# A graph-attention and mixture-of-experts kernel: the tridiagonal recursion inside the chunks in four pair products instead of eight steps

## What is computed

```python
v = jnp.clip(ffn_out @ Wv + bv, -V_MAX, V_MAX)      # one value for each of the 128 nodes
# diagonal of (T - i)^-1, T tridiagonal with v on the diagonal and 1 beside it:
#   a_i = d_i - 1/a_{i-1} (forwards), b_i = d_i - 1/b_{i+1} (backwards), d_i = v_i - 1j
#   G_ii = 1 / (a_i + b_i - d_i)
gr, gi = _bk_gii(v)
feats = jnp.clip(jnp.stack([gr, gi], -1) * mask[..., None], -FEAT_CLAMP, FEAT_CLAMP)
return ffn_out + bk_scale * (feats @ Wo + bo)
```

## Time and profile before

| | us |
|---|---|
| median of 3 runs | 501.85 |
| lowest and highest run | 500.89, 502.28 |
| the profiled execution, its time | 502.62 |
| the profiled execution, span from first to last instruction | 500.8 |
| TensorE busy | 466.2 (93%) |
| VectorE busy | 136.2 (27%) |
| bytes read from HBM | 189.62 MB, 379 GB/s over the span |

### The profile page before, as it was taken

One profiled execution on the slowest core, in us unless ns is written; L12 is line 12 of the kernel. 1 busy time (PEld: TensorE's weight loads), 2 busy tenths in 40 slices (PEclk: granted clock), 3 DMA queues, 4 the chain that ended last, 5 costly groups with the idle time before them and its releaser, 6 DMA issues.

```text
span 500.8 us, 5998 instructions
## 1 busy us (share of the span) xinstructions
PE 466.2 (93%) x2292; PEld 232.7 (46%) x2292; DVE 136.2 (27%) x362; ACT 62.1 (12%) x119; POOL 32.9 (7%) x52
## 2 busy tenths in 40 slices
PE   7999999999998999999999999999898889789892
PEld 6666665666556344344344344353243234224352
DVE  6673697437105311010010010010010011001165
ACT  1010222002003120020020020020020011002100
POOL 3242220000100000121000000000000000000000
PEclk9999999999998999999999999999999999999996
DMA  8889999999999699899999999999999999999800
GB/s 309 309 285 403 402 401 417 413 401 411 426 425 370 237 407 375 338 417 420 425 428 423 422 427 427 423 421 430 424 424 424 425 425 423 425 425 424 347 1 31
DMA packets 32541, 190.22 MB, mean 380 GB/s; under 512 B 5423, under 2 KB 5631, under 8 KB 18190
## 3 DMA queue, kind: packets, MB, share of 16 engines
q1 hardware_dynamic: 31694, 189.94, 93.2%
q0 software_dynamic: 544, 0.05, 0.1%
q10 hardware_dynamic: 288, 0.03, 0.0%
HBM read 189.62 MB, written 0.39 MB: 379 GB/s over the span
## 4 chain that ended last, share of the span: by engine, by line
PE 58%; DMA 22%; SPq 13%; DVE 5%; issue 2%; ACT 0%; DVEq 0%
PE ps L1300 16%; DMA chunk<-in_L_ffn_W 14%; PE ps L1273 14%; PE ps L1099 11%; PE ps L1059 6%; DMA lower<-in_L_ffn_W 6%; SPq L333 5%; SPq L323 4%; SPq L328 3%; PE ps L1286 2%; PE ps L1087 2%; DMA slot<-in_L_gnn_W 2%; PE ps L1114 2%; PE ps L1235 2%; SPq L347 1%
## 5 line engine op out<-in xcount | busy, mean ns | idle before, releaser
L1300 PE MATMUL ps<-lower,hidden 128*64 128x384 f32 x516 | 88.6, 490 | 5.3 <-DMA lower<-in_L_ffn_W 5.3
L1273 PE MATMUL ps<-chunk,gathered 128*64 128x512 f32 x324 | 73.5, 598 | 7.3 <-DMA chunk<-in_L_ffn_W 7.3
L1059 PE MATMUL ps<-slot,xT 128*128 128x384 f32 x192 | 64.0, 487 | 0.2 <-DMA slot<-in_L_gnn_W 0.2
L1273 PE MATMUL ps<-extra,gathered 128*64 128x512 f32 x252 | 57.6, 597 | 6.1 <-DMA extra<-in_L_ffn_W 5.9
L1300 PEld LDWEIGHTS ps<-lower,hidden 128*64 128x64 f32 x516 | 35.9, 137 | 51.2 <-issue 40.6
L1099 PE MATMUL ps<-slot,eluT 128*128 128x384 f32 x168 | 55.3, 486 | 0.0
L884 DVE TENSOR_TENSOR hidden<-ps,b_T 128x384 f32<-128x384 f32 x32 | 17.1, 555 | 129.8 <-PE ps L1286 129.8
L1059 PEld LDWEIGHTS ps<-slot,xT 128*128 128x128 f32 x192 | 35.6, 190 | 22.8 <-issue 0.3
L1273 PEld LDWEIGHTS ps<-chunk,gathered 128*64 128x64 f32 x324 | 21.7, 136 | 50.6 <-issue 36.7
L1300 PE MATMUL ps<-lower_on,hidden 128*64 128x384 f32 x252 | 43.7, 492 | 0.0
L1099 PEld LDWEIGHTS ps<-slot,eluT 128*128 128x128 f32 x168 | 31.5, 190 | 20.7
(11 more groups left out here) (303 smaller groups left out, 287.1 us busy)
## 6 DMA issues: line engine op xcount, KB each, us to landing
lower<-in_L_ffn_W SPq DMA_DIRECT2D x43, 1152.0 KB, 23.1
chunk<-in_L_ffn_W SPq DMA_DIRECT2D x27, 1536.0 KB, 19.7
slot<-in_L_gnn_W SPq DMA_DIRECT2D x31, 1152.0 KB, 15.6
extra<-in_L_ffn_W SPq DMA_DIRECT2D x21, 1536.0 KB, 25.1
lower_on<-in_L_ffn_W SPq DMA_DIRECT2D x21, 1152.0 KB, 28.7
slot<-in_L_gnn_W SPq DMA_DIRECT2D x3, 384.0 KB, 4.8
x_sb<-in_x SPq DMA_DIRECT2D x1, 384.0 KB, 3.4
out<-xc SPq DMA_DIRECT2D x1, 384.0 KB, 2.3
```

The costliest lines, as they stand in the source:

```text
L1059: last = T.matmul(ps[:, 2 * (h % 2) + b, 0:HB], xT[:, 3 * half + k, :], slots[n % RING][:, k, b * HB:(b + 1) * HB], start=(n % 2 == 0 and ...
L1273: last = T.matmul(ps[b * CAP:(b + 1) * CAP, s, 0:BANK], gathered[:, k, :], upper_homes[k][:, at:at + BANK], start=(k == 0), stop=(k == KT ...
L1300: last = T.matmul(ps[c * CAP:(c + 1) * CAP, 4, 0:HB], hidden[:, q, k, b, :], lower_homes[i][:, k, c * HB:(c + 1) * HB], start=(i == 0 and ...
```

## The change

The tile `cf_w` shrinks from 40 to 8 elements a row. Row pairs of it now hold a 4x4 state matrix: pair 0 is the identity, written by GpSimd. For each pair of steps a 4x4 matrix K is built from the two values v0 and v1, in `cf_k` (4 matrices of 16): its constant entries are set by GpSimd's MEMSETs, its other entries by six VectorE instructions, each for all four pairs at once. Then three times a product (TENSOR_TENSOR, 48 x 64, broadcast over four) and a sum (TENSOR_REDUCE to 48 x 16) multiply K on the state; state 1 is the first K itself, copied into `cf_w` while the first product runs. The wait on `cf_init` goes from 3 to 4. `WARM[10]`, the number of identity products ahead of L1380, goes from 8 to 2.

```diff
--- before.py
+++ after.py
@@ -55,7 +55,7 @@
 LOADS = CHUNKS + DOWN
 EARLY = 3
 ATONCE = 6
-WARM = (3, 5, 2, 2, 2, 0, 1, 3, 2, 0, 8, 12)
+WARM = (3, 5, 2, 2, 2, 0, 1, 3, 2, 0, 2, 12)
 
 
 def gnn_moe_kernel(nc, x, src, dst, gw1, gas1, gad1, gb1, gw2, gas2, gad2, gb2,
@@ -127,15 +127,15 @@
         wo_rows = place("wo_rows", [P, 2, D])
         wv_row = place("wv_row", [P, D])
         top[0] = moe_base + lower_at[7]
-        tail_tiles = [("cf_w", [CP, CL + 2, 4 * (CL + 2)]), ("cf_v", [CP, CL]), ("cf_t", [CP, 4 * (CL + 2)]),
+        tail_tiles = [("cf_w", [CP, CL + 2, 8]), ("cf_v", [CP, CL]), ("cf_t", [CP, 4, 4, 4]),
               ("cf_m", [CP, CH, 16]), ("cf_mm", [2, CH, 16]), ("cf_s", [2, CH, 4]), ("cf_x", [2, 4, 4]),
               ("cf_n", [2, CH]), ("cf_p", [CP, CH, 4]), ("cf_b", [CP, 4]), ("cf_y", [CP, CL + 1, 2, 4]),
               ("cf_th", [CP, CL + 1, 2]), ("cf_q", [CP, 3, CL, 2]), ("cf_r", [CP, CL]), ("cf_a", [CP, CL, 2]),
               ("cf_d", [CH, CL, 2]), ("cf_c", [CH, CL, 2]), ("cf_g", [CH, CL, 2]), ("cf_e", [CH, CL]),
               ("cf_f", [P, CL, 2]), ("cf_pre", [2, GC, GC, 4, 4]), ("cf_px", [2, GC, 4, 2, 4]),
-              ("cf_sx", [2, GC, GC - 1, 4, 4])]
+              ("cf_sx", [2, GC, GC - 1, 4, 4]), ("cf_k", [CP, CL // 2, 16]), ("cf_h", [CP, CL // 2])]
         (cf_w, cf_v, cf_t, cf_m, cf_mm, cf_s, cf_x, cf_n, cf_p, cf_b, cf_y, cf_th, cf_q, cf_r, cf_a,
-         cf_d, cf_c, cf_g, cf_e, cf_f, cf_pre, cf_px, cf_sx) = [place(*t) for t in tail_tiles]
+         cf_d, cf_c, cf_g, cf_e, cf_f, cf_pre, cf_px, cf_sx, cf_k, cf_h) = [place(*t) for t in tail_tiles]
         assert top[0] <= moe_base + lower_at[7] + slot
         top[0] = after_moe
 
@@ -449,13 +449,14 @@
                 pool.dma_start(wo_rows[0:1, j, :], wo[j:j + 1, :]).then_inc(end_rows_in, 16)
             pool.dma_start(wv_row[0:1, :], wv).then_inc(end_rows_in, 16)
             G.memset(cf_w[:, 0:2, :], 0.0).then_inc(cf_init, 1)
+            G.memset(cf_k[:, :, :], 0.0).then_inc(cf_init, 1)
             G.memset(cf_s[:, 0, :], 0.0).then_inc(cf_init, 1)
             G.memset(cf_d[:, :, 1], -1.0)
-            pool.wait_ge(cf_init, 2)
-            for at in range(2):
-                for row, sign in ((0, 1.0), (1, 1.0), (2, -1.0), (3, -1.0)):
-                    first = 4 * row + 2 * at + row % 2
-                    G.memset(cf_w[:, at, first::16], sign)
+            pool.wait_ge(cf_init, 3)
+            G.memset(cf_w[:, 0:2, :].rearrange("p s m -> p (s m)")[:, 0::5], 1.0)
+            G.memset(cf_k[:, :, 0:6:5], -1.0)
+            G.memset(cf_k[:, :, 6:10:3], -1.0)
+            G.memset(cf_k[:, :, 3:13:9], 1.0)
             G.memset(cf_s[:, 0, 0:1], 1.0 / FAR)
             G.memset(cf_s[:, 0, 2:3], 1.0).then_inc(cf_init, 1)
 
@@ -922,14 +923,31 @@
             V.scalar_tensor_tensor(out=v_steps[:, :], in0=ps[:, 3, 0:1].to_broadcast([P, CL]), scalar=col(VBASE),
                                    in1=step_mask[:, :], op0=ALU.add, op1=ALU.mult).then_inc(v_ready, 1)
 
-            dve.wait_ge(cf_init, 3)
+            dve.wait_ge(cf_init, 4)
             dve.wait_ge(v_turned, 1)
             step(V.tensor_scalar(cf_v[:, :], ps[0:CP, 2, 0:CL], VMAX, -VMAX, ALU.min, ALU.max))
-            for i in range(CL):
-                n = 4 * (CL + 1 - i)
-                step(V.tensor_tensor(cf_t[:, 0:n], cf_w[:, i + 1, 4:4 + n], cf_w[:, i, 0:n], ALU.subtract))
-                step(V.scalar_tensor_tensor(out=cf_w[:, i + 2, 0:n], in0=cf_w[:, i + 1, 0:n],
-                                            scalar=cf_v[:, i:i + 1], in1=cf_t[:, 0:n], op0=ALU.mult, op1=ALU.add))
+            pair = [CP, CL // 2, 2]
+            v0, v1 = cf_v[:, 0:CL:2], cf_v[:, 1:CL:2]
+            V.tensor_tensor(cf_h[:, :], v0, v1, ALU.mult)
+            V.tensor_copy(cf_k[:, :, 2:8:5], v0.unsqueeze(2).to_broadcast(pair))
+            V.tensor_scalar(cf_k[:, :, 8:14:5], v1.unsqueeze(2).to_broadcast(pair), -1.0, None, ALU.mult)
+            V.tensor_tensor(cf_k[:, :, 11], v0, v1, ALU.add)
+            step(V.scalar_tensor_tensor(out=cf_k[:, :, 14], in0=v0, scalar=-1.0, in1=v1, op0=ALU.mult,
+                                        op1=ALU.subtract))
+            step(V.tensor_scalar(cf_k[:, :, 10:16:5], cf_h[:, :].unsqueeze(2).to_broadcast(pair), -2.0, None, ALU.add))
+            flat = cf_w[:, :, :].rearrange("p s m -> p (s m)")
+            for i in range(1, CL // 2):
+                state = cf_k[:, 0, :] if i == 1 else flat[:, 16 * i:16 * (i + 1)]
+                ins = V.tensor_tensor(cf_t[:, :, :, :],
+                                      cf_k[:, i, :].rearrange("p (o k) -> p o k", o=4).unsqueeze(2)
+                                      .to_broadcast([CP, 4, 4, 4]),
+                                      state.rearrange("p (k c) -> p c k", k=4).unsqueeze(1)
+                                      .to_broadcast([CP, 4, 4, 4]), ALU.mult)
+                if i == 1:
+                    V.tensor_copy(flat[:, 16:32], cf_k[:, 0, :])
+                step(ins)
+                step(V.reduce_sum(flat[:, 16 * (i + 1):16 * (i + 2)],
+                                  cf_t[:, :, :, :].rearrange("p o c k -> p (o c) k"), AX))
 
             V.tensor_tensor(cf_m[:, :, :].rearrange("p c (a b) -> p c a b", a=2),
                             cf_w[:, CL:CL + 2, 0:8].unsqueeze(1).to_broadcast([CP, CH, 2, 8]),
```

## The result

The changed kernel takes **500.41 us** in the median of 20 runs (498.75 to 501.78); the kernel before, beside it, 502.06 us (500.2 to 502.68, 20 runs). The ratio is 0.9969, with a 95% interval of 0.9961 to 0.9978: faster by 0.31%, which is 1.56 us (the two medians themselves lie 1.65 apart). The forecast was 500.4 us and 1.45 us less. The size was met; of the two verdicts at the bound of 0.3%, between which the prediction saw nearly a toss, the estimate falls just on the faster side, and its interval covers both.

A forecast was written before the change was run, and what follows sets the result against it. After the weight stream, a chain of short VectorE and TensorE instructions bounds the end. Matrices 0.76 plus products 1.59 make 2.35 us in place of 3.80: 1.45 less, 501.85 to 500.4 us; range 499.3 to 501.5.

The forecast's parts named there:

- the bound of 0.3%: About 0.3%, 1.5 us, is what a measurement can tell from no change; chances 0.43 faster, 0.53 within, 0.04 slower.
- The place: The recursion, 479.70 to L934's start at 483.50, lies on the chain of waits: 3.80 us on the path, no cover.
- Rival D: The recursion is not what L934 waits for, so the time would be 501.85 us; chance 0.01.
- The unwaited four: First four VectorE instructions making the matrices, no wait between them: 4 x 0.08 = 0.32 us, after L983 to L985.
- Rival B: Unwaited instructions cost a full turn, 0.19 not 0.08, and the copy 0.19: gain 0.8 us, 501.0; chance 0.08.
- The fifth instruction: A waited SCALAR_TENSOR_TENSOR in making the matrices, priced as the last L931 (48x8): 0.25 us.
- The sixth: A waited TENSOR_SCALAR, last in making the matrices, priced as L927: 0.19 us.
- The products: Three pairs on VectorE, each a product of 0.29 us reading at a distance and a sum of 0.24: 1.59 us.
- The copy at nothing: Copy of state 1 into `cf_w`, issued between first product and its sum: 0 us, bounds 0 and 0.08.
- WARM[10] as the condition: Identity matmuls ahead of L1380: with 16, 1.2 us of gain lost; with four, 0.51 us, TensorE free 0.3 early.
- Rival A: Gain 1.6 us or more, from cheaper distant reads or fifth instruction, and L1397's clock; all together 1.9, 500.0; chance 0.27.
- Rival C: TensorE's clock falls earlier with fewer identity matmuls, making it 2.2 us late at L1389: 1.2 us slower, 503.1; chance 0.03.

## Why the prediction was right

The gain came by the forecast's mechanism and sum. That 500.4 met 500.41 to the hundredth is luck: the forecast counted from 501.85, the median of three runs, where the twenty beside the changed kernel gave 502.06, and the gain was larger than 1.45 by 0.1 (from the ratio) to 0.2 (from the medians).

Step by step, by its own terms:

- **The place.** That the recursion stands alone on the chain was right: 1.50 us less in it gave 1.53 less in the tail. Rival D is out.
- **The unwaited four** were priced at 0.32 from L983 to L985 and took 0.30. Rival B (a full turn each) had put 0.44 more on them; with waits the recursion is indeed 0.50 longer, without them it is not.
- **The fifth instruction** is the term that was mis-sized: 0.25 taken from the last L931, 0.18 measured. The row was taken for its operation and width, but it reads its scalar per partition. The constant in place of the value shows that this is 0.06 us, which the new instruction, with a constant, does not have. The sixth took 0.20 (0.19).
- **The products** were 1.59 and took 1.62: 0.54 a turn, of which the product and its wait are the 0.29 forecast and the sum 0.25, not 0.24. The price for reading at a distance, from L947, was right for the right reason.
- **The copy at nothing** was right: the sum stands 0.29 us behind the product with the copy (479.57 to 479.86) and also without it (480.11 to 480.40).
- **WARM[10] as the condition** was right, 1.2 us lost without it predicted and 1.17 measured (1.22 less the usual 0.05). But four of the identity matmuls were counted as a linear share, 0.51; the row has 0.71, as a fixed part does not shrink with the count. So they ended 0.05 us before `cf_m` (481.56 and 481.61) and not 0.3 before it: the condition held, by less than was thought.
- **Rival A** had half its mechanism: the fifth instruction did cost no more than a waited TENSOR_SCALAR. Reading at a distance was not cheaper, and the clock at L1397 gave nothing: L1415 took 0.60 as before. The level's fall did not stay where it was while the work moved up, as the rival had it; it came at 491.21, 1.17 us ahead of L1415 (492.38). Making the matrices took 0.08 us less than forecast and the products 0.03 more, so the recursion gave 1.50 instead of 1.45, and the tail 1.53, right at the bound.
- **Rival C** did not come. Its premise, that with fewer identity products the level falls ahead of the 24 and stays low, was seen in none of the eight profiles with WARM[10] at 2. In five the level fell near the start of the 24, from 0.02 us ahead of it to 0.73 behind (the changed kernel, 484.39; before it had been 0.28 behind), and rose again 3.4 us later, before L1407; the 24 still ended 0.2 us before VectorE's result. In three it stayed high past these products. Its price for a late TensorE is of the right kind, as WARM[10] at 8 shows at the other place; at L1389 it was not shown.

The point left uncertain was which side of 0.3% the result falls on. The terms that were off, by 0.08 and 0.03, are as large as the forecast's distance from that bound, 0.05, and the last weights land at times that differ by 3 us from one execution to the next, so that even twenty runs leave the side open.

## What to carry to other kernels

A chain of tiny operations is priced by its waits: in this kernel 0.19 to 0.28 us for each waited instruction of 4 to 36 elements a partition, and 0.07 to 0.09 for an unwaited one of up to 16. So batch the independent ones ahead of a single wait, and let a dependent one wait for its own source alone. When such a chain is shortened, look at what the other engine has queued ahead of the meeting point, and shorten that until it ends first again. And read a gain of this size from a stretch of the trace with a fixed start, since the span carries the scatter of what lies before it.

## What the runs showed of the hardware that was not expected

- A SCALAR_TENSOR_TENSOR with a scalar read per partition lasts 0.06 us longer than the same with a constant (220 against 157 ns at 48x8).
- At the high clock level 4, 16, 24 and 40 identity matmuls of 128x128 in a row took 0.71, 2.05, 2.94 and 4.73 us: 0.26 us and 0.112 for each. The 0.128 of the prediction, from 16, holds a part of the fixed 0.26.
- Of two profiles of the same kernel, one has a stretch of 3.4 us at the low clock level amid 24 back-to-back matmuls and one has none, which makes their length 4.57 or 2.94 us.
